# The last residual add of a Mamba and MoE block, shared between GpSimd and VectorE

## The reference

```python
x = x + _layernorm(_L0_attn_ref(_layernorm(x)))   # RMS norm, in-projection, gate, causal conv of 4 taps,
                                                  # selective scan with 16 states over 512 channels, out-projection
x = x + _layernorm(_L0_ffn_ref(_layernorm(x)))    # 8 experts, top 2 of them by gate logits, and a shared expert
return x
```

## Time and profile before

| | |
|---|---|
| median of 3 runs | 1755.47 us (1754.18 to 1758.54) |
| the profiled execution's own time | 1749.59 us |
| its span, from first to last instruction | 1747.5 us |
| third stage within it, from its first load | 1711.1 to 1747.5 us, 36.4 us |
| VectorE, ScalarE, GpSimd busy in that stage | 24.3, 19.1, 16.8 us |
| 16 DMA engines, mean busy share in that stage | 0.69 |

### The profile page before, as it was taken

The page is one execution under the profiler, slowest core; times in us unless marked ns, Lnnn a source line. Parts: engine busy times, 40 slices in busy tenths (PEclk is TensorE's granted clock), DMA queues, the critical chain, the costliest instruction groups (busy, mean ns, idle before and its releaser), DMA issues.

```text
span 1747.5 us, 23922 instructions
## 1 busy us (share of the span) xinstructions
PE 1538.8 (88%) x7068; PEld 1036.1 (59%) x7068; DVE 1149.9 (66%) x1928; ACT 852.6 (49%) x1480; POOL 1046.2 (60%) x1233
## 2 busy tenths in 40 slices
PE   5888799998999998989997676899999999999990
PEld 2354555655645645646555555576777777777770
DVE  2199999899999898999999993222222222222225
ACT  3566668668668677677576562211112112112124
POOL 0578879879889899799799873322222222222224
PEclk9899899999999999999999787999999999999995
DMA  3111111320211211211114626214122112122116
GB/s 112 33 52 35 51 56 44 101 62 33 84 61 49 80 50 49 76 53 58 56 47 133 214 73 202 76 33 128 31 35 35 33 33 35 32 34 35 31 29 198
DMA packets 84394, 116.21 MB, mean 67 GB/s; under 512 B 11121, under 2 KB 58577, under 8 KB 84273
## 3 DMA queue, kind: packets, MB, share of 16 engines
q1 hardware_dynamic: 63344, 82.94, 15.3%
q0 software_dynamic: 16704, 27.57, 8.0%
q10 hardware_dynamic: 4224, 4.19, 0.7%
HBM read 81.05 MB, written 33.10 MB: 65 GB/s over the span
## 4 chain that ended last, share of the span: by engine, by line
PE 36%; POOL 7%; DVE 4%; issue 4%; ACT 2%; DMA 1%; POOLq 0%; DVEq 0%; ACTq 0%; SPq 0%
PE A L1254 10%; PE bA L1213 9%; PE bH L1213 9%; POOL arena L1018 4%; DVE arena L861 2%; PE bY L1237 2%; DVE arena_t L878 1%; PE A L1245 1%; DMA sum_scratch<-arena_t 1%; PE A L1237 1%; POOL expert_in_scratch L1006 1%; PE A L554 1%; PE A L563 1%; PE bH L591 0%; PE A L576 0%
## 5 line engine op out<-in xcount | busy, mean ns | idle before, releaser
L1018 POOL TENSOR_TENSOR arena<-arena 128x512 f32<-128x512 f32 x512 | 644.2, 1276 | 99.9 <-DVE arena L861 97.6
L735 ACT ACTIVATE bA<-arena,a_neg 128x512 f32<-128x512 f32 x512 | 352.0, 691 | 258.6 <-DVE arena L861 256.3
L591 PEld LDWEIGHTS bH<-ident,arena 128*128 128x128 f32 x2048 | 246.4, 145 | 303.6 <-DVE arena L861 139.6
L591 PE MATMUL bH<-ident,arena 128*128 128x128 f32 x2048 | 325.5, 286 | 95.2 <-DVE arena L861 73.3
L861 DVE TENSOR_TENSOR_SCAN arena<-bA,arena 128x512 f32<-128x512 f32 x256 | 305.3, 1208 | 63.2 <-ACT bA L735 48.1
L861 DVE TENSOR_TENSOR_SCAN arena<-bA,hl,arena 128x512 f32<-128x512 f32 x256 | 320.7, 1267 | 3.9 <-ACT bA L735 2.0
L1349 POOL DMA_INDIRECT sum_scratch<-arena_t x71 | 113.6, 1599 | 188.8 <-issue 161.1
L1385 ACT ACTIVATE arena_t<-bA 128x352 f32<-128x352 f32 x142 | 58.1, 461 | 323.9 <-PE bA L1213 323.9
L1254 PE MATMUL A<-arena,hT 128*128 x852 | 197.5, 382 | 0.8 <-ACT hT L1391 0.8
L1343 POOL DMA_DIRECT2D arena_t<-expert_in_scratch x71 | 40.7, 574 | 256.3 <-PE A L1245 205.4
L1213 PE MATMUL bA<-arena,arena_t 128*128 x568 | 179.9, 459 | 1.3 <-ACT arena_t L1396 1.3
(11 more groups left out here) (194 smaller groups left out, 2068.1 us busy)
## 6 DMA issues: line engine op xcount, KB each, us to landing
arena<-b_scratch SPq DMA_DIRECT2D x128, 256.0 KB, 3.2
arena_t<-expert_in_scratch POOLq DMA_DIRECT2D x71, 132.0 KB, 2.4
arena<-in_L_ffn_Wg_dram SPq DMA_DIRECT2D x8, 704.0 KB, 5.4
arena<-in_L_ffn_Wu_dram SPq DMA_DIRECT2D x8, 704.0 KB, 6.9
arena<-in_L_ffn_Wd_dram SPq DMA_DIRECT2D x8, 640.0 KB, 8.0
arena<-in_L_attn_x_dram SPq DMA_DIRECT2D x8, 512.0 KB, 5.0
arena_x<-in_L_attn_x_dram SPq DMA_DIRECT2D x8, 512.0 KB, 5.0
x_scratch<-arena_x SPq DMA_DIRECT2D x8, 512.0 KB, 3.2
```

The costliest lines, as they stand in the source:

```text
L591: i = e.transpose(bH[g % NH][:, q * P:(q + 1) * P], hh[:, (n - 1) % 2, q, d * P:(d + 1) * P], ident[:])
L735: e.activation(bA[g % NA][:], dt[c % 2][:, d, :], ACT.Exp, scale=a_neg[:, d, n:n + 1]).then_inc(s_a, 1)
L1018: e.tensor_tensor(bb[:, k % NB, :], u[c % 2][:, d, :], br[:, n % NR, :], ALU.mult).then_inc(s_bb, 1)
```

## The change

VectorE's two adds of 128x512 for a unit become one add of 128x512 on VectorE, of the unit's first two rows per partition, and one of the same size on GpSimd, of the other two. Both come from one function, `half_out(e, u, h, s_)`. VectorE's waits for rows 0 and 1 (`s_no3` at 4u + 2), GpSimd's for rows 2 and 3 (4u + 4). GpSimd's loop gets two more rounds: its add of unit u−2 stands behind `pool_stats` of unit u, and the adds of units 6 and 7 come at the end. GpSimd's adds raise a semaphore of their own, `s_op`, and SyncE's queue waits for both semaphores before it writes a unit. GpSimd's adds also wait for the loads of `x1` (`s_x1u`).

```diff
-    s_no3 = sem("s_no3"); s_o = sem("s_o")
+    s_no3 = sem("s_no3"); s_o = sem("s_o"); s_op = sem("s_op")
...
-    def dve_out(e, u):
+
+    def half_out(e, u, h, s_):
         e.wait_ge(s_x1u, 16 * NU)
-        for q in range(UT):
-            if q % 2 == 0:
-                e.wait_ge(s_no3, UT * u + q + 2)
-                e.tensor_tensor(x1s[:, u, q:q + 2, :].rearrange("p j d -> p (j d)"), x1s[:, u, q:q + 2, :].rearrange("p j d -> p (j d)"),
-                                acc[:, u, q:q + 2, :].rearrange("p j d -> p (j d)"), ALU.add).then_inc(s_o, 1)
+        n = UT // 2
+        e.wait_ge(s_no3, UT * u + (h + 1) * n)
+        e.tensor_tensor(x1s[:, u, h * n:(h + 1) * n, :].rearrange("p j d -> p (j d)"), x1s[:, u, h * n:(h + 1) * n, :].rearrange("p j d -> p (j d)"),
+                        acc[:, u, h * n:(h + 1) * n, :].rearrange("p j d -> p (j d)"), ALU.add).then_inc(s_, 1)
...
         for u in range(NU):
-            e.wait_ge(s_o, UT // 2 * (u + 1))
+            e.wait_ge(s_o, u + 1)
+            e.wait_ge(s_op, u + 1)
             e.dma_start(unit_rows(out_rows, u), x1s[:, u, :, :]).then_inc(s_out, 16)
...
-        for u in range(NU):
-            pool_stats(e, u)
+        for u in range(NU + 2):
+            if u < NU:
+                pool_stats(e, u)
+            if u >= 2:
+                half_out(e, u - 2, 1, s_op)
...
             if u >= 2:
-                dve_out(e, u - 2)
+                half_out(e, u - 2, 0, s_o)
```

## The result

The changed kernel takes 1761.44 us (median of 13 runs, 1756.44 to 1765.78) against 1755.47 us for the kernel before (median of 13 runs, 1753.07 to 1758.54). The ratio is 1.0034, with a 95% interval of 1.0023 to 1.0045: slower by about 6 us, as forecast in direction and size (1762.2 predicted, 6.7 us of loss). The profiled execution took 1761.25 us.

What follows compares the result with a forecast made beforehand. The prediction took GpSimd's chain of small steps to bound the last stage. Its terms, 5.0 − 0.4 + 1.9 + 0.2 = +6.7 us on the median of 1755.47, gave 1762.2 us, range 1758.0 to 1766.0.

Steps and rivals of the forecast that it cites:

- GpSimd's chain is the bound, VectorE is not: Last stage: GpSimd's small steps set the 3.22 us period; VectorE's removed 0.69 us a unit is worth nothing by itself.
- Period: Last stage, va to va: from 3.22 to 4.22 us, +1.00, over five periods +5.0 us.
- The stretch of `va`: GpSimd's va, from the third unit on: −0.36 us each, six of them, as the VectorE add beside it goes.
- The extra wait: GpSimd, in front of its long add: one more wait already come true, some 0.08 us, bounds 0 and 0.16.
- L138's stretch stays: GpSimd's small step L138 beside VectorE's first-half add: still 0.72 us where it takes 0.20 alone.
- Rival 1: L138's stretch goes away: units 3 to 8 save 0.52 us each, total +3.6, 1759.1 us; chance 0.22.
- Last `va`: GpSimd's va of the last unit is no longer stretched: −0.4 us.
- Tail: After the last L140: three GpSimd adds back to back, excluding VectorE's last add, 4.69 us against 2.83, +1.9.
- Transfers and end: Output transfers: the last two come 1.28 us apart, so the last queues, +0.2 us.
- Rival 2: VectorE's add falls on GpSimd's long add in each unit, stretching it by 0.69: +3.5 over five periods, 1765.7 us; chance 0.08.
- Rival 3: GpSimd's add is hidden, only the six va stretches are saved: −2.2 us, 1753.3 us; chance 0.02.

Runs made afterwards that it cites:

- e2: The kernel before with VectorE's second add of each unit left out and nothing in its place; ratio to before 0.9990, stage 33.3 us against 36.4.
- e3: The changed kernel with a second GpSimd add of 128x512 behind each of its adds, written to unused space; ratio to before 1.0096.
- e1: The changed kernel with VectorE's half add left out; ratio to before 1.0023, stage 38.9 us against the changed kernel's 43.0.
- e6: The kernel before with a GpSimd memset of 128x4 behind everything, waiting for VectorE's last add; ratio to before 1.0003, stage 37.9 us against 36.4.
- e5: The changed kernel with both halves of units 6 and 7 added on VectorE; ratio to before 1.0048, stage 42.2 us.
- e4: The changed kernel with GpSimd's add moved between va and the Newton steps, into the wait for ScalarE's root; ratio to before 1.0018, stage 39.4 us.

## Why the prediction was right, step by step

The direction, the mechanism and the total were right, but that the total came so close is in part luck: period and tail were put 1.3 us too high together, the end 1.0 us too low, and the errors cancelled. For the profiled execution by itself 1756.3 us was predicted and 1761.25 measured, with 5.5 us of its growth ahead of the stage.

- **GpSimd's chain is the bound, VectorE is not.** Shown by e2 (2.87, not 2.5) and e3 (+1.20 of period for +1.23 of add). VectorE was near, though: with two adds it sat idle only 0.22 us a unit.
- **Period: +1.00 predicted, +0.86 measured**, over five periods 4.3 us against 5.0. The stretch of `va` went as forecast (0.55 to 0.19). From L140 to the next `va` pass 1.50 us where 0.28 passed before, so the add with its waits costs 1.22, not 1.36. The extra wait costs nothing: the add starts 0.15 us after L140's start, before L140's recorded end.
- **L138's stretch stays: right**, seven units at 0.72. VectorE's add comes 0.03 us ahead of it in the new period, where it waits for ScalarE. In the old steady period it didn't: it followed VectorE's own statistics without a wait and met L138 to within 0.01 us, so the prediction's reason, that both starts hang on one ScalarE step, holds for the new period only. Rival 1 is out, and e1 prices it at 0.52 a unit.
- **Last `va`: −0.4 predicted, −0.35 measured.**
- **Tail: +1.9 predicted, +1.3 measured.** The exclusion between the two engines' adds is real, but it cost GpSimd 0.44 us, not 0.69: VectorE's add, released 1.2 us earlier, ended only 0.54 us behind GpSimd's second one. e1, without it, has a tail 0.37 shorter. The rest is the wait that costs nothing and adds that follow each other every 1.22 us.
- **Transfers and end: +0.2 predicted, +1.2 measured.** Queueing was as small as forecast: from the last issue to the landing 3.1 us (1755.1 to 1758.2) against 2.9 before. The step that failed is that nothing else can end the span. GpSimd's drain, 4.4 us, ends it, as e6 shows by itself. Without the drain the changed kernel would, by e5, have ended 0.8 us behind its landing and not 1.5 (1758.16 to 1759.63), so I estimate that the drain has some 0.7 of the 1.2 us, queueing 0.2, and SyncE's later last steps the rest.

The measured terms are 4.3 − 0.35 + 1.3 + 1.2 = 6.5 us, and 0.1 us of noise ahead of the third `va`: 6.6 in the stage, 6.0 in the medians. Rival 2, VectorE's add on GpSimd's long add in each unit, occurred in the last unit only. Rival 3 needed a hidden add; e4 shows what hiding is worth at the one place tried, 0.48 us a unit, out of a wait of 0.56.

Two readings of the prediction were off and changed nothing. The 512 instructions of the earlier trace rows are products, not adds; GpSimd's adds of that shape took 1.26 to 1.27 us, products 1.28. And not every output before went without queueing: the first took 4.1 us to landing, while the last loads were still coming.

The end of the changed kernel also settles what no row of before showed, a VectorE add released beside a running GpSimd add: it waits for its end, 1.76 us in place of 0.69. SBUF — State Buffer, section Who interferes with whom, in the Trainium skill says that a VectorE instruction with two SBUF inputs contends with a GpSimd one that reads SBUF, that the shared ports are an exclusive lock, and that the order of issue decides who blocks. The trace agrees, in both orders: 0.72 for 0.20 us with VectorE ahead, 1.76 for 0.69 with GpSimd ahead. Where the two recorded starts lie within 0.01 us of each other, GpSimd's step was the one that waited.

## What to carry to other kernels

Before moving work off a busy engine, look for the engine whose instructions follow each other without a wait in the chain: here the busiest engine of the stage was not the bound, and the one that took the work was. Price the removal by what it does to that engine (0.35 us a unit) and not by its own length (0.69). Then look at what is last: on which engine the last instruction stands, and how many outputs it holds back, since what ends the program late cost 1.2 to 3.9 us here, beside the 4.3 us of the five longer periods.

## What the runs showed of the hardware

GpSimd's drain at the end of the program ended 4.4 us after its last instruction in every profile, be that an add of 1.71 us or a memset of 0.10. In the five profiles where it was the last to end (the changed kernel, e1, e3, e4, e6), the span ended 0.2 us behind it. VectorE's drain ended with its last add, within 0.1 us. An output of 512 KB moved in 1.5 us at some 345 GB/s and needed 2.9 us to landing; three issued within 1.7 us of each other added 1.3 us to the wait for the last one (e5).
